# The DFT over the tokens, from high and low parts

## The reference

```python
h = depthwise_conv(x, 7 taps) + b_dw            # along the frames
h = relu(einsum("od,bds->bos", w_pw, h) + b_pw) # pointwise over the channels
h = max_over_pairs_of_frames(h)                 # 750 frames -> 375 tokens
y = real(fft2(h))                               # over 375 tokens and 192 channels
h = layernorm(y) * gamma + beta
h = h + attention(layernorm(h))
h = h + feed_forward(layernorm(h))              # routed attention or a mix, then an MLP
```

## Time and profile before

| | |
|---|---|
| three runs | 634.43, 630.13, 632.99 us; median 632.99 |
| profiled execution, time | 630.36 us |
| profiled execution, span from the first to the last instruction | 628.5 us |
| mean granted clock of PE | 0.938 |
| busy | PE 537.3 us (85%), DVE 444.2 (71%), ACT 234.6 (37%), POOL 68.4 (11%) |
| one step of the loop | 66.6 us |

### The profile page before, as it was taken

The page is one execution under the profiler, slowest core; times in us unless marked ns, Lnnn a source line. Parts: engine busy times, 40 slices in busy tenths (PEclk is TensorE's granted clock), DMA queues, the critical chain, the costliest instruction groups (busy, mean ns, idle before and its releaser), DMA issues.

```text
span 628.5 us, 9490 instructions
## 1 busy us (share of the span) xinstructions
PE 537.3 (85%) x3344; PEld 441.9 (70%) x3344; DVE 444.2 (71%) x1239; ACT 234.6 (37%) x619; POOL 68.4 (11%) x67
## 2 busy tenths in 40 slices
PE   1637588969998999999999999899989998959896
PEld 1425476848776977787877887687779776847676
DVE  5777577577877887888778887788778573853240
ACT  1124022621465145702581157214651457013611
POOL 0010011002020022002100301030201220020000
PEclk9987598688999999999999999999999999977699
DMA  8421000010001000000001000100000000000001
GB/s 215 143 63 38 0 2 1 1 37 2 1 1 37 18 3 2 21 17 18 0 0 37 18 0 0 37 18 0 0 0 19 1 1 1 2 19 1 1 7 31
DMA packets 8217, 12.73 MB, mean 20 GB/s; under 512 B 1896, under 2 KB 6722, under 8 KB 8189
## 3 DMA queue, kind: packets, MB, share of 16 engines
q1 hardware_dynamic: 8189, 12.37, 7.3%
HBM read 10.07 MB, written 2.30 MB: 20 GB/s over the span
## 4 chain that ended last, share of the span: by engine, by line
PE 58%; DVE 21%; ACT 12%; issue 6%; DMA 1%; POOL 1%; DVEq 0%; ACTq 0%; SPq 0%; POOLq 0%
PE xb L1163 8%; PE yb L1078 7%; PE zb L1078 7%; PE xb L1108 5%; PE yb L1340 5%; ACT probs L967 3%; PE xb L1117 3%; ACT w_sq L892 2%; PE xb L1078 2%; DVE dw L401 2%; DVE nr L557 2%; ACT w_s L891 2%; DVE w_sq L508 2%; PE xb L1144 2%; DVE junk L516 2%
## 5 line engine op out<-in xcount | busy, mean ns | idle before, releaser
L815 POOL TENSOR_TENSOR rs<-ve,half 125x3 f32<-125x3 f32 (+1 forms) x32 | 33.4, 1045 | 529.3 <-DVE ve L366 451.7
L383 DVE SCALAR_TENSOR_TENSOR dw<-x_in,w_dw_sb,dw 96x750 f32<-96x750 f32 x84 | 79.0, 990 | 0.2
L1078 PE MATMUL xb<-xhT,w_qkv_sb 96*128 96x376 f32 x288 | 64.0, 368 | 4.8 <-DVE xhT L468 3.4
L1078 PE MATMUL yb<-n2T,w_sb 96*128 96x376 f32 x288 | 60.2, 350 | 4.2 <-DVE n2T L703 3.2
L1078 PEld LDWEIGHTS xb<-xhT,w_qkv_sb 96*128 96x128 f32 x288 | 52.7, 206 | 11.3 <-DVE xhT L468 6.8
L1163 PE MATMUL xb<-scratch,w_sq 128*125 128x192 f32 x288 | 52.7, 346 | 5.2 <-ACT scratch L903 5.2
L1163 PEld LDWEIGHTS xb<-scratch,w_sq 128*125 128x125 f32 x288 | 51.3, 202 | 5.8 <-DVE scratch L530 5.8
L1078 PEld LDWEIGHTS yb<-n2T,w_sb 96*128 96x128 f32 x288 | 49.1, 191 | 6.9 <-DVE n2T L703 4.2
L1340 PE MATMUL yb<-w_sb,gelu 128*125 128x192 f32 x252 | 48.7, 336 | 5.3 <-ACT probs L967 5.3
L1340 PEld LDWEIGHTS yb<-w_sb,gelu 128*125 128x125 f32 x252 | 40.3, 187 | 10.5 <-ACT probs L967 6.5
L972 ACT ACTIVATE probsT<-zb 125x384 f32<-125x384 f32 x48 | 26.4, 549 | 24.0 <-PE zb L1274 24.0
(11 more groups left out here) (190 smaller groups left out, 1122.1 us busy)
## 6 DMA issues: line engine op xcount, KB each, us to landing
x_in<-in_x SPq DMA_DIRECT2D x8, 567.0 KB, 4.2
out<-res_f SPq DMA_DIRECT2D x7, 281.2 KB
probsT<-in_w_qkv SPq DMA_DIRECT2D x1, 576.0 KB, 7.1
w_out_sb<-in_w_out SPq DMA_DIRECT2D x1, 576.0 KB
w_sb<-in_w SPq DMA_DIRECT2D x1, 576.0 KB
probsT<-in_w SPq DMA_DIRECT2D x1, 576.0 KB, 4.2
rows_sb<-in_rows SPq DMA_DIRECT2D x1, 504.0 KB
dft_n_sb<-in_dft_n SPq DMA_DIRECT2D x1, 493.5 KB
```

The source lines that it names most:

```text
L383: ins = dve.scalar_tensor_tensor(out=dw[0:C, c, :], in0=src, scalar=w_dw[:, c, k:k + 1], in1=dw[0:C, c, :], op0=ALU.mult, op1=ALU.add)
L815: pool.tensor_tensor(out_[:], in_[:], half3[:] if len(in_.shape) == 3 else half3[:, 0, :], ALU.pow).then_inc(rs.sem, 1)
L1078: ins = mm(o, a[:, k], b[:, l], start=start and k + l == 0, stop=stop and k == 1)
```

## The change

`dft_n` gets a high and a low part, `dft_parts`, made once in step 0: ACT copies it to fp32r ahead of its first `relu`, DVE subtracts ahead of its first `pool_pairs`. In every step ACT copies each pooled tile to fp32r behind its `relu` calls (`pooled_high`), DVE subtracts the copies from the pooled tiles behind `pool_pairs`. `over_tokens` waits for the three high parts and runs 12 products with them (both parts of the table), then waits for the low parts and runs 6 with the table's high part: 18 products of 376 columns in place of 6 in fp32.

```diff
+        dft_parts = sb("dft_parts", [P, 2, T, 2 * KF], fp32r)
...
+        pooled_parts = sb("pooled_parts", [P, 2, T, D], fp32r)
...
+        dft_high, dft_low = signal("dft_high"), signal("dft_low")
+        pool_high, pool_low = signal("pool_high", T), signal("pool_low", T)
...
             def pool_pairs(b):
 
-                if not first(b):
+                if first(b):
+                    dve.wait_ge(dft_high.sem, 1)
+                    dve.tensor_tensor(dft_parts[:, 1], dft_n[:], dft_parts[:, 0], ALU.subtract).then_inc(dft_low.sem, 1)
+                else:
                     dve.wait_ge(*fa_ready.before(b))
                 for t in range(T):
                     dve.wait_ge(*relu_done.of(b, t + 1))
                     src = frames(t)
                     dve.scalar_tensor_tensor(out=pooled_h[:, t, :], in0=src[:, D:2 * D], scalar=0.0, in1=even[:, t, :],
                                              op0=ALU.max, op1=ALU.max).then_inc(pool_done.sem, 1)
+                for t in range(T):
+                    dve.wait_ge(*pool_high.of(b, t + 1))
+                    dve.tensor_tensor(pooled_parts[:, 1, t, :], pooled_h[:, t, :], pooled_parts[:, 0, t, :], ALU.subtract)\
+                       .then_inc(pool_low.sem, 1)
...
+            def pooled_high(b):
+                if not first(b):
+                    act.wait_ge(*fa_ready.before(b))
+                for t in range(T):
+                    act.wait_ge(*pool_done.of(b, t + 1))
+                    act.activation(pooled_parts[:, 0, t, :], pooled_h[:, t, :], ACT.Copy).then_inc(pool_high.sem, 1)
...
             def step(p, q, r, w):
                 front, middle, last = p is not None, q is not None, r is not None
+                if first(p):
+                    act.wait_ge(dft_in.sem, DFT)
+                    act.activation(dft_parts[:, 0], dft_n[:], ACT.Copy).then_inc(dft_high.sem, 1)
                 if front:
                     relu(p)
+                    pooled_high(p)
...
             def over_tokens(b):
                 if first(b):
                     pe.wait_ge(dft_in.sem, DFT)
-                pe.wait_ge(*pool_done.of(b))
+                pe.wait_ge(*pool_high.of(b))
+                if first(b):
+                    pe.wait_ge(dft_low.sem, 1)
+                for c in range(CT):
+                    for l in range(2):
+                        for t in range(T):
+                            mm(xb[0:C, c, 0:2 * KF], pooled_parts[:, 0, t, chan(c)], dft_parts[:, l, t, :], start=(t + l == 0), stop=False)
+                pe.wait_ge(*pool_low.of(b))
                 for c in range(CT):
                     for t in range(T):
-                        ins = mm(xb[0:C, c, 0:2 * KF], pooled_h[:, t, chan(c)], dft_n[:, t, :], start=(t == 0), stop=(t == T - 1))
+                        ins = mm(xb[0:C, c, 0:2 * KF], pooled_parts[:, 1, t, chan(c)], dft_parts[:, 0, t, :], start=False, stop=(t == T - 1))
                 ins.then_inc(fa_ready.sem, 1)
```

## The result

| | before | after |
|---|---|---|
| median, 20 executions each | 631.65 us | 640.23 us |
| lowest, highest | 629.83, 645.94 | 632.47, 649.10 |
| ratio after / before | | 1.0099, 95% interval 1.0070 to 1.0127 |
| profiled execution, time (span) | 630.36 (628.5) | 643.56 (641.6) |
| mean granted clock in it | 0.938 | 0.896 |

The changed kernel is slower by 1%. I had forecast 629, and 623 to 636. The ratio leaves out executions over 1.5% above their kernel's fastest; the medians don't, and the profile of after is one of its longer executions, so I use it for places, and the experiments for sizes.

What follows compares the result with a forecast made beforehand. The prediction took a PE-led chain of waits, with the token DFT on it in all eight passes, as the bound. Seven passes at 0.31 us plus 0.4 in the first gave 2.6 us: 629 us, range 623 to 636.

Steps and rivals of the forecast that it cites:

- Pitch of a product: DFT on PE: 18 fp32r products at 0.171 us each, 3.08 us instead of 3.79, saving 0.71 us a pass.
- PE's start: Hand-over before the DFT: PE waits for ACT's three high copies, first DFT load 0.40 us later, bounds 0.36 to 0.60.
- nT and the taps: DVE beside the DFT: added subtractions shrink both slacks to 0.7 and 0.6 us, so DVE's share costs nothing.
- A pass of the loop: Each loop pass: 0.71 us saved less 0.40 of delay, net 0.31 us, between -0.25 and 0.6.
- The first pass's products: DFT of the first pass: 5.1 us instead of 6.24; the pass taken to end 0.4 us sooner.
- The table's parts: First pass: ACT's copy of about 1.1 us and DVE's subtraction of 1.3 us, both hidden by existing waits.
- the clock falls in the longer gap: Rival at PE's pause before the DFT: clock halves once a pass, 1.55 us each; 639 to 642 us, chance 0.06.
- a single idle stretch at 1.00: Argument against a clock fall: PE was idle from 126.15 to 128.60 us with the granted clock at 1.00.
- one lucky case: Rival, early clock recovers: one early stretch at 0.50 doesn't come, 6.3 us saved; 621 to 624 us, chance 0.10.
- The collision: Rival on DVE between pool and nT: subtractions collide with GpSimd, keys wait, 1.2 us a pass; 638 to 641, chance 0.07.
- no-gain: Rival at the DFT: the hand-over takes all that the products save; 631 to 634 us, chance 0.23.
- no-cheaper: Rival at the DFT: 18 products cost what fp32 records cost, 5.7 us, a pass 2.3 us longer; 648 us, chance 0.02.

Runs made afterwards that it cites:

- after_warm: The changed kernel plus extra unused products on PE in long pauses of steps 0, 1 and 8, pause ahead of the DFT kept; 620.04 us, 0.9821 of before.
- gap_warm: The kernel before, its fp32 DFT waiting for high and low parts made but unused, plus extra unused products in steps 0, 1 and 8; 624.15 us, 0.9872 of before.

## Why the prediction was wrong

**The work was sized right.** Pitch of a product: forecast 0.171, 0.167 measured. Copy 0.359, 0.353 measured over 24; subtraction 0.354, 0.354; PE's start 0.40 late, 0.38. nT and the taps kept their slack: 0.91 and 0.69 us, forecast 0.7 and 0.6. A pass of the loop gains 0.28 where no fall comes, forecast 0.31. The first pass's products took 5.06 us (26.27 to 31.33), forecast 5.1. The table's parts were hidden: the subtraction of 1.32 us ended before the third pool, which still waited 1.60 us.

**The step that failed** is the rival "the clock falls in the longer gap", which I gave 0.06. Its mechanism, place and price were those measured: 1.55 a fall forecast, 1.5 to 1.6 between steps with and without (67.85 to 66.25). What I argued against it was a single idle stretch at 1.00, as if the same pause always did the same. It doesn't: in the profile of after the same pause of 0.38 or 0.39 us behind the same transposes let the clock fall in three steps and not in the two that follow; in after_warm it was two, in gap_warm two. A stretch that once did no harm bounds nothing. That the median, 640.23, lies in this rival's 639 to 642 is luck: it was drawn with a fall in every pass, the profile has three, and most of the excess stands elsewhere. The Trainium skill's sentence that I weighed there (TensorE: Matmul & The Clock Gate, section "Part 4: PE-mode transpose"), that transposes don't count as PE-busy in the same way, made the pause 2.56 us. The runs agree with it in so far as 0.4 us behind the transposes were enough where 1.3 us stood ahead of them, and two products there, or a shorter pause ahead, kept the clock up; none of them replaced the transposes by other work.

**The term that was missing** is the clock outside the loop. I took the stretches at 0.50 in steps 0, 1, 8 and 9 as given and let them enter only as one lucky case. They are the largest variable of this kernel, and in the profile of after the larger part of the error: 9.8 of the 13.1 us more stand in steps 0 to 2 and behind step 7. Over 52 executions of the kernel before, beside the experiments, the time is 600.2 us + 0.35 us for each us at 0.50 (correlation 0.99), from 629.5 at 79 us to 646.8 at 133. The changed kernel's 20 executions give 597.7 us + 0.36 (correlation 0.94). They have 96 to 143 us of it, median 115, which the line puts at 639.2 (640.23 measured), while before's median of 631.65 stands at 91 on its own line. The 24 us between, at 0.36, are 8.6; less the 2.6 of the work this makes 6 of the 8.6 us measured. The lines can't place the rest: the changed kernel has no execution under 96 us, so that where its line meets no time at 0.50 is uncertain by some 4 us (standard error). In its profile the loop's three falls are 10 of the 55 us more, the rest stands in the early steps and the last two.

**What stays open.** That the last two steps' time goes with the clock is shown by the line through the 13 profiles. Why the changed kernel meets the long stretch there in most of its executions, and the kernel before in fewer, is not: one profile for each kernel shows 27 to 65 us there, and no run moved the steps against the clock's changes by a chosen amount. I believe that any shift of the start does this; it wasn't tried. The kernel before meets it too: 19 of the 52 executions took over 640 us, 6 of 12 in one set, whose median of 639.01 is near the changed kernel's; of the 20 here it was one. So how much slower the changed kernel's median is depends on the set, and which passes of the loop fall is open as well.

**The other rivals.** The collision came, in single steps of other kernels and from GpSimd's side (a late addition): the keys waited 0.40 us for nT, and the step was shorter all the same. The no-gain and the no-cheaper cases are out by the pitch and the start.

## What to carry to other kernels

A wait of 0.4 us on TensorE's path can cost its length, or 1.5 us on top where the clock falls behind it: price it with the clock, look at what TensorE did just before, and close it (begin with the first tile that is ready) before counting the cheaper products behind it. One profile at full clock isn't evidence that a pause is harmless; ask for the clock of many executions. Where executions differ by more than the change is worth, take that cause away in both kernels and compare those.

## What the runs showed of the hardware

- The clock stayed at 0.50 for 51.20 us in after's last two steps, with PE busy for 43.99 of them.
- Products without use, in pauses, gave the kernel before 2.5% (631.85 to 615.69 us, beside each other).
- Two VectorE instructions in a row changed places as the one that waits for GpSimd: three instructions of nr took 3.3 or 1.06 us, three subtractions 0.90 or 2.54, and an addition of GpSimd 1.44 or 2.42. The Trainium skill (SBUF — State Buffer, section "SBUF: two separate sides") names the shared port pair for it; the durations agree.
- Three partial products of fp32r parts cost 0.50 us (3 x 0.167) where one fp32 product of the same 376 columns cost 0.63 (2 x 0.315).
